# Channel mix on one core: the hidden layer's matmuls go ahead of the gate's, and the squares move from ScalarE to VectorE

## What is computed

```python
xc = _ln(x, ln2_g, ln2_b)
xx2 = _shift(xc)
xk2 = xc * cm_k + xx2 * (1 - cm_k)
xr2 = xc * cm_r + xx2 * (1 - cm_r)
kk = jnp.square(jax.nn.relu(jnp.einsum('btc,hc->bth', xk2, ffn_Wk)))
kv = jnp.einsum('bth,ch->btc', kk, ffn_Wv)
rkv = jax.nn.sigmoid(jnp.einsum('btc,oc->bto', xr2, ffn_Wr)) * kv
return x + rkv
```

## Time and profile before

| what | us |
|---|---|
| median of three executions | 1672.6 |
| the profiled execution's own time | 1671.31 |
| its span in the trace | 1669.5 |
| outside the span (the difference) | 1.8 |
| PE busy, share of the span | 88% |
| channel mix, first transpose to last matmul, in the trace | 1522.1 to 1637.7 |

### The profile page before, as it was taken

The page is one execution under the profiler, slowest core; times in us unless marked ns, Lnnn a source line. Parts: engine busy times, 40 slices in busy tenths (PEclk is TensorE's granted clock), DMA queues, the critical chain, the costliest instruction groups (busy, mean ns, idle before and its releaser), DMA issues. The chain is left out here.

```text
span 1669.5 us, 26535 instructions
## 1 busy us (share of the span) xinstructions
PE 1467.1 (88%) x11120; PEld 1056.9 (63%) x11120; DVE 750.1 (45%) x1317; ACT 474.2 (28%) x788; POOL 555.9 (33%) x315
## 2 busy tenths in 40 slices
PE   7778977477988999999999999999998897828996
PEld 3556754243444778778787787877877574413773
DVE  2455289989435342332313323133231313994733
ACT  0323201041111115243252432424324351402612
POOL 6101057656323042132121321213214233534911
PEclk9779965688998999999999999999999998867997
DMA  6300030010101411111011110111102116003000
GB/s 236 151 1 1 9 130 1 0 70 0 76 0 57 155 52 58 39 44 53 27 58 52 33 53 25 58 52 34 53 31 70 43 58 258 1 0 120 1 1 26
DMA packets 50101, 91.29 MB, mean 55 GB/s; under 512 B 28600, under 2 KB 41664, under 8 KB 46912
## 3 DMA queue, kind: packets, MB, share of 16 engines
q1 hardware_dynamic: 49984, 89.60, 15.2%
HBM read 79.89 MB, written 9.70 MB: 54 GB/s over the span
## 5 line engine op out<-in xcount | busy, mean ns | idle before, releaser
L1074 POOL TENSOR_TENSOR ctx_hi<-ctx_raw,one 128x1536 fp32r<-128x1536 f32 (+1 forms) x36 | 102.9, 2858 | 619.6 <-DMA ctx_raw<-in_ctx 427.8
L1328 DVE TENSOR_TENSOR V<-PS,vbias 128x512 f32<-128x512 f32 (+1 forms) x104 | 71.9, 691 | 339.6 <-PE PS L1114 339.5
L1256 ACT COPY ET<-PS 128x512 f32<-128x512 f32 (+1 forms) x224 | 129.6, 585 | 300.4 <-PE PS L1170 296.7
L1359 DVE TENSOR_SCALAR_CACHE_REDUCE E<-PS 128x384 f32<-128x384 f32 (+1 forms) x256 | 131.8, 571 | 159.6 <-PE PS L1147 159.0
L1170 PE MATMUL PS<-ident,E 128*128 128x128 f32 (+1 forms) x832 | 127.3, 278 | 8.8 <-ACT ET L1256 8.8
L1077 POOL TENSOR_TENSOR ctx_raw_r<-ctx_raw,ctx_hi 128x1536 fp32r<-128x1536 f32 (+1 forms) x36 | 131.1, 3641 | 2.8
L1114 PE MATMUL PS<-ctx_raw_r,wk_hi 128*128 128x384 f32 (+1 forms) x512 | 128.6, 355 | 0.0
L1114 PE MATMUL PS<-wv_lo,ctx_hi 128*128 128x512 f32 (+1 forms) x416 | 126.7, 407 | 0.0
L1114 PE MATMUL PS<-ctx_hi,wk_hi 128*128 128x384 f32 (+1 forms) x512 | 122.9, 361 | 2.4 <-POOL ctx_raw_r L1077 2.4
L1263 ACT ACTIVATE E<-E,peak 128x1601 f32<-128x1601 f32 x64 | 103.5, 1623 | 64.8 <-DVE peak L1364 64.8
L1114 PE MATMUL PS<-wv_hi,ctx_hi 128*128 128x512 f32 (+1 forms) x416 | 120.7, 412 | 0.8 <-issue 0.8
(11 more groups left out here) (283 smaller groups left out, 2357.1 us busy)
## 6 DMA issues: line engine op xcount, KB each, us to landing
ctx_raw<-in_ctx SPq DMA_DIRECT2D x27, 768.0 KB, 4.4
ctx_raw<-in_ctx_first SPq DMA_DIRECT2D x9, 900.0 KB, 4.7
rel_scr<-rel_out SPq DMA_DIRECT2D x8, 640.0 KB, 3.7
fwk<-in_fwk SPq DMA_DIRECT2D x1, 4096.0 KB, 25.8
fwv<-in_fwv SPq DMA_DIRECT2D x1, 4096.0 KB, 12.7
corr<-rel_scr SPq DMA_DIRECT2D x64, 48.0 KB
p_scr<-E SPq DMA_DIRECT2D x16, 192.0 KB, 2.3
near<-p_scr SPq DMA_DIRECT2D x64, 48.0 KB
```

Source lines behind the costliest of these rows:

```text
L1074: nc.gpsimd.tensor_tensor(ctx_hi[r][:, :, 0:n], ctx_raw[r][:, :, 0:n], one[:].unsqueeze(1).broadcast_to([P, KC, n]), ALU.mult).then_inc(S[ ...
L1256: nc.scalar.copy(ET[0:n, j % ET_RING, :], src[0:n, :]).then_inc(S["et_out"], 1)
L1328: v.tensor_tensor(V[0:rows, at % V_RING, :], bank(4 + NUMBER[unit] % 2)[0:rows, :], vbias[0:rows, :], ALU.add).then_inc(S["v_out"], 1)
L1359: v.tensor_scalar(E[:, p, k0:k0 + n], bank(r)[:, 0:n], 1.0, None, ALU.mult, ALU.max, accum_out=tops[:, p, c:c + 1]).then_inc(S["s_out"], 1)
```

## The change

On TensorE the gate's product moves from ahead of the hidden loop to behind it, and now waits for `mixed` at 2 KC. The value product waits for all of `h_lo` ahead of its first matmul, where it waited for `h_hi` there and for `h_lo` before its third part. On VectorE `xk` is mixed first, and `xr` after the rest of `xk`. ScalarE squares no more: VectorE multiplies `hidden` by itself in place, ScalarE rounds that to `hidden_hi` with a copy, and VectorE subtracts, as before. The four sigmoids come last on ScalarE. The hidden loop thus has three VectorE instructions in each turn where it had two, and three on ScalarE where it had four.

```diff
--- before.py
+++ after.py
@@ -1704,11 +1704,6 @@
         @block.tensor
         def _(pe):
             tr.tensor(pe, nm)
-            pe.wait_ge(s.loaded["fwr"], 16)
-            pe.wait_ge(S["mixed"], KC)
-            pe.wait_ge(tr.ready, KC)
-            for t in range(NT):
-                linear_to_tokens(nc, bank(t), flat(xr[:]), t, s.fwr, 0, D).then_inc(S["r_ps"], 1)
             pe.wait_ge(S["x_lo"], KC)
             for g in range(HC):
                 pe.wait_ge(S["k_lo"], g + 1)
@@ -1720,13 +1715,16 @@
                         last = nc.tensor.matmul(bank(4 + g % 4), w[:, g, c, :], flat(x)[:, c], start=(k == 0), stop=(k == 3 * KC - 1))
                         k += 1
                 last.then_inc(S["h_ps"], 1)
+            pe.wait_ge(s.loaded["fwr"], 16)
+            pe.wait_ge(S["mixed"], 2 * KC)
+            pe.wait_ge(tr.ready, KC)
+            for t in range(NT):
+                linear_to_tokens(nc, bank(t), flat(xr[:]), t, s.fwr, 0, D).then_inc(S["r_ps"], 1)
             pe.wait_ge(S["v_split"], 2 * HC)
-            pe.wait_ge(S["h_hi"], HC)
+            pe.wait_ge(S["h_lo"], HC)
             for t in range(NT):
                 k = 0
                 for x, w in ((hidden_hi, fwv_hi[:]), (hidden_hi, fwv_lo[:]), (hidden_lo, fwv_hi[:])):
-                    if k == 2 * HC:
-                        pe.wait_ge(S["h_lo"], HC)
                     for g in range(HC):
                         last = nc.tensor.matmul(bank(4 + t), x[:, g, t * P:(t + 1) * P], w[:, g, :], start=(k == 0), stop=(k == 3 * HC - 1))
                         k += 1
@@ -1740,34 +1738,26 @@
             def key_weights(g):
                 nc.scalar.copy(fwk_hi[:, g], fwk[:, g]).then_inc(S["k_hi"], 1)
 
-            def squared_high(g):
-                act.wait_ge(S["relu"], g + 1)
-                nc.scalar.activation(hidden_hi[:, g], hidden[:, g], ACT.Square).then_inc(S["h_hi"], 1)
-
-            def square(g):
-                act.wait_ge(S["h_hi"], g + 1)
-                nc.scalar.activation(hidden[:, g], hidden[:, g], ACT.Square).then_inc(S["squared"], 1)
+            def round_hidden(g):
+                act.wait_ge(S["squared"], g + 1)
+                nc.scalar.copy(hidden_hi[:, g], hidden[:, g]).then_inc(S["h_hi"], 1)
 
             for g in range(AHEAD):
                 key_weights(g)
             for c in range(KC):
-                act.wait_ge(S["mixed"], KC + c + 1)
+                act.wait_ge(S["mixed"], c + 1)
                 nc.scalar.copy(xk_hi[:, c], xk[:, c]).then_inc(S["x_hi"], 1)
-            for t in range(NT):
-                act.wait_ge(S["r_ps"], t + 1)
-                nc.scalar.activation(gate[:, t, :], bank(t), ACT.Sigmoid).then_inc(S["gate_in"], 1)
             for g in range(HC):
                 if g + AHEAD < HC:
                     key_weights(g + AHEAD)
                 act.wait_ge(S["h_ps"], g + 1)
                 nc.scalar.activation(hidden[:, g], bank(4 + g % 4), ACT.Relu).then_inc(S["relu"], 1)
                 if g >= 1:
-                    squared_high(g - 1)
-                if g >= 2:
-                    square(g - 2)
-            squared_high(HC - 1)
-            square(HC - 2)
-            square(HC - 1)
+                    round_hidden(g - 1)
+            round_hidden(HC - 1)
+            for t in range(NT):
+                act.wait_ge(S["r_ps"], t + 1)
+                nc.scalar.activation(gate[:, t, :], bank(t), ACT.Sigmoid).then_inc(S["gate_in"], 1)
 
         @block.vector
         def _(dve):
@@ -1779,24 +1769,25 @@
                 v.tensor_tensor(fwk_lo[:, g], fwk[:, g], fwk_hi[:, g].bitcast(F32), ALU.subtract).then_inc(S["k_lo"], 1)
 
             def rest_of_hidden(g):
-                dve.wait_ge(S["squared"], g + 1)
+                dve.wait_ge(S["h_hi"], g + 1)
                 v.tensor_tensor(hidden_lo[:, g], hidden[:, g], hidden_hi[:, g].bitcast(F32), ALU.subtract).then_inc(S["h_lo"], 1)
 
             dve.wait_ge(tr.turned, KC)
-            tr.vector(dve, xa, diff, ((vec("cm_r"), xr),), S["mixed"])
             tr.vector(dve, xa, diff, ((vec("cm_k"), xk),), S["mixed"])
             for g in range(AHEAD):
                 key_weights(g)
             for c in range(KC):
                 dve.wait_ge(S["x_hi"], c + 1)
                 v.tensor_tensor(xk_lo[:, c], xk[:, c], xk_hi[:, c].bitcast(F32), ALU.subtract).then_inc(S["x_lo"], 1)
+            tr.vector(dve, xa, diff, ((vec("cm_r"), xr),), S["mixed"])
             for g in range(HC):
                 if g + AHEAD < HC:
                     key_weights(g + AHEAD)
-                if g >= 3:
-                    rest_of_hidden(g - 3)
-            for g in range(HC - 3, HC):
-                rest_of_hidden(g)
+                dve.wait_ge(S["relu"], g + 1)
+                v.tensor_tensor(hidden[:, g], hidden[:, g], hidden[:, g], ALU.mult).then_inc(S["squared"], 1)
+                if g >= 1:
+                    rest_of_hidden(g - 1)
+            rest_of_hidden(HC - 1)
             for t in range(NT):
                 out = flat(y[:])[:, t]
                 dve.wait_ge(S["kv_ps"], t + 1)
```

## The result

The changed kernel takes 1689.45 us, the median of four executions (1686.55 to 1689.85), against 1673.03 for the kernel before in the same runs (1671.31 to 1673.77). The ratio is 1.0097, with a 95% interval from 1.0083 to 1.0112: 16.4 us slower, where 14.6 were forecast (1687.2 us).

What follows compares the result with a forecast made beforehand. PE was taken as the bound, the value product's start telling all: 4.8 (start) + 13.8 (loop) - 1.7 (gate's cold passes) - 2.3 (old wait) = 14.6 us, giving 1687.2 us. Forecast 1684 to 1690 (0.69), range 1679 to 1692.

Steps and rivals of the forecast that it cites:

- The bound: PE's timeline: the whole change is told by how far the value product's start moves from 1593.49, 14.6 us later.
- the loop: Hidden loop: PE waits for key-weight rests from group 9 on; it takes 59.1 us instead of 45.3, 13.8 more.
- the old wait: Ahead of the value product: PE's 2.33 us wait for the last rounding is covered by the gate's product.
- The start of the loop: First matmul of the hidden loop at 1535.2, behind the last `xk_lo`; PE idles 4.8 us more than before.
- The cold start: Start of the hidden loop: low clock for 4.3 us, 0.466 a matmul, group 0 ending at 1540.1.
- Whether GpSimd gets in ahead of the late mixings: VectorE's late mixings ahead of the loop: GpSimd getting in first was part of the forecast's spread, 2.3 us.
- The square and the alternation: Hidden loop: VectorE's squares alternate with GpSimd at 1.575 us; a turn takes 4.73, 32 instructions 50.4.
- The clock in the waiting part: Rival, chance 0.13: PE's clock falls while it waits in the loop, up to 7.3 us more, 1689 to 1694.5.
- The gate: Gate's product behind the loop: high clock throughout, 13.8 us instead of 15.5, ending at 1608.1.
- GpSimd was not kept out: Rival, chance 0.08: VectorE's denser turns keep GpSimd out, the value product waits for `v_split`, 8.5 us later, 1681.1.
- the square does take part in the alternation: Rival, chance 0.08: squares run beside GpSimd at 0.60, value product 3.6 us late, 1676.2, or 1674.9 with PE only bound.
- there was overlap all along: Rival, no overlap, chance 0.02: VectorE and GpSimd instructions cost 1.77 together, 32 of them 6.2 us more, 1693.4.

Runs made afterwards that it cites:

- order alone: Changed kernel with the squares back on ScalarE, so only the order of TensorE, mixings and sigmoids differs from the kernel before: 1673.53 us, ratio 1.0004.
- squares alone: Kernel before with the squares on VectorE and nothing else changed, the gate's product staying ahead of the loop: 1683.23 us, ratio 1.0063.
- its wait filled: Changed kernel with six unused matmuls added in PE's wait for `xk_lo` ahead of the hidden loop: 1689.52 us, ratio 1.0100.
- The two fills: Unused matmuls in PE's wait: six ahead of the changed kernel's loop, ratio 1.0100; three ahead of the gate in the kernel before, ratio 1.0001.

## Why the prediction was right, step by step

*The bound.* Right: one number, the start of the value product, carried the change, 15.87 us of it against a forecast of 14.6. Term by term: the start 4.8 us as forecast, the loop 15.6 instead of 13.8, the gate's product 2.2 less instead of 1.7, the old wait 2.3 less as forecast. So the loop was sized 1.8 us too low, and the miss in the gate hid 0.5 of that. The median, 1689.45, lies in the forecast of 1684 to 1690, but only 0.55 inside its upper end.

*The start of the loop.* Forecast 13.1 us behind the first transpose (1535.2 - 1522.08), measured 13.06.

*The cold start.* Under-sized: all of group 0 and the start of group 1 ran at the low clock, not 4.3 us of it, and group 0 took 5.28 us instead of 4.9. A matmul at the low clock cost 0.44 (5.28 / 12), and 0.43 from start to start behind the first four, not 0.466. It cost nothing in the end: the first ReLU was done 19.2 us behind the first transpose, and the first square started at 20.6, behind the late mixings.

*Whether GpSimd gets in ahead of the late mixings.* I let VectorE make them undisturbed and named the other case with 2.3 us. It was the other case: four mixings in 6.3 us, and the first square at 20.6 instead of 18.7. Moving the mixings away brought the end of the loop 3.2 us forward and the value product 1.6.

*The square and the alternation.* Right, and shown by three runs: 32 instructions in 50.0 us where 50.4 and 0.3 were forecast; 0.60 each and no wait of PE with GpSimd out of the way; and no cost with one input in SBUF. PE waited from group 9 on, as worked out. The rest for group 15 came at 70.6 where 69.4 was forecast.

*The clock in the waiting part.* A rival with 0.13, it came true in one group of six: group 14 took 4.44 instead of 2.79, of which 0.5 counted, since the rest for group 15 was late anyway. The other waiting groups ran at the full clock. The prediction had named a clock that falls in the loop's second half as a sign that it is wrong. That sign came, but small: one turn and 0.5 us, where the rival had priced six turns and a cold gate at up to 7.3.

*The gate.* 13.3 us behind the loop against 13.8, at the full clock; no gap ahead of the value product, with `h_lo` and the splits (62.7 us behind the first transpose) long done.

*The rivals.* GpSimd was not kept out; the square does take part in the alternation; there was overlap all along. With one factor from PSUM the square did stay out of it, and the time, 1674.49, is close to the 1674.9 to 1676.2 that this rival had been priced at. The prediction did not say that the order alone is free and the squares alone are not, nor that the two hang together. That came out of the runs.

## What to carry to other kernels

Before an elementwise instruction is moved to VectorE, look at what GpSimd does at that time and at how many inputs in SBUF the instruction has: here the same square made a turn 1.6 us longer or not at all. Count what a busy engine's row of instructions needs from its first to its last, and compare that with PE's turn times the number of turns, head start included. A product that fills PE's wait for others is worth leaving there; behind the loop it covers only the gap that is there, so move as much of it as the gap is long.

## What the runs showed of the hardware beyond that

A GpSimd split that arrives while VectorE makes a row of subtractions stands behind the whole row (3.78 us before, 3.92 with the squares alone), but one that arrived at its end was in at once and slowed the mixings behind it (1.10, changed kernel). What decides that wasn't tried. In the three other kernels whose PE waited in turns of 4.6 to 5.1 us (squares alone, and the changed kernel with its wait filled or with `xr` mixed in the loop) the clock also fell: once in group 13 (squares alone), once in group 14 (`xr` mixed in the loop), and twice with the wait filled, in group 11, the third that PE waited for, and in group 14. The waits ahead of those groups were 1.7 to 2.0 us long, shorter than the gap of 2.33 that left the clock up in the kernel before. What decides between them stays open. The two fills differed in what they left open ahead of the work: with 1.59 us between the two the gate began at the full clock, with 3.83 the loop began at the low one.
